# Eight-stream GNN stack on one core: masks of two score banks move from TensorE to VectorE, engine orders rewritten, loop unrolled

## What is computed

```python
h = jnp.maximum(_layernorm(x), 0.0); x = x + _L0_gnn_ref(h, ..., adj)   # masked attention, 8 heads of 32
h = jnp.maximum(_layernorm(x), 0.0); x = x + _L1_gnn_ref(h, adj, ...)   # (adj.T * q k^T) / row norm, times v
h = jnp.maximum(_layernorm(x), 0.0); x = x + _L2_gnn_ref(h, ..., adj)   # graph attention, softmax, elu
h = jnp.maximum(_layernorm(x), 0.0); x = x + _L3_gnn_ref(h, adj, ...)   # adj @ h @ w + bias
# inside L0:
attn = jnp.einsum('bhnd,bhmd->bhnm', q, k) * scale
attn = jnp.where(attn_mask[None, None] == 0, -jnp.inf, attn)
attn = jax.nn.softmax(attn, axis=-1)
o = o @ w_proj + b_proj; ...; return o + layernorm(o) * gamma + beta
```

## Time and profile before

| | us |
|---|---|
| median of 3 runs | 1529.49 |
| lowest and highest | 1529.12, 1531.04 |
| the profiled execution: its time | 1527.43 |
| the profiled execution: span, first to last instruction | 1525.4 |
| PE, DVE, ACT, POOL busy (share of the span) | 97%, 85%, 73%, 43% |

### The profile page before, as it was taken

How to read it: one execution, slowest core, us unless ns; L and a number is a source line. 1 busy time by engine, 2 the same in 40 slices (tenths; PEclk the granted TensorE clock), 3 DMA queues, 4 the chain that set the end, 5 groups by cost and what they waited for, 6 DMA issues and landing times.

```text
span 1525.4 us, 46270 instructions
## 1 busy us (share of the span) xinstructions
PE 1482.7 (97%) x16392; PEld 1375.0 (90%) x16392; DVE 1301.0 (85%) x3726; ACT 1120.1 (73%) x2884; POOL 661.3 (43%) x981
## 2 busy tenths in 40 slices
PE   6989999999999999999989999999999999999996
PEld 5879999999999999999989999999999999999985
DVE  3888888888888888888888898898898898898895
ACT  4667777777777777777767777777777777777763
POOL 2244444444444444444444444444444444444442
PEclk9999999999999999999999999999999999999999
DMA  3000010000000010000010010010000010000001
GB/s 107 15 16 15 23 30 22 23 29 22 23 30 22 23 29 22 23 29 23 23 31 18 28 29 18 27 30 18 28 30 19 26 30 20 25 29 22 17 16 35
DMA packets 38102, 39.84 MB, mean 26 GB/s; under 512 B 2416, under 2 KB 37488, under 8 KB 37872
## 3 DMA queue, kind: packets, MB, share of 16 engines
q1 hardware_dynamic: 37872, 36.84, 7.9%
HBM read 20.05 MB, written 16.78 MB: 24 GB/s over the span
## 4 chain that ended last, share of the span: by engine, by line
PE 94%; DVE 2%; issue 2%; ACT 1%; POOL 1%; DMA 0%; POOLq 0%; DVEq 0%; ACTq 0%
PE bank L325 41%; PE mid L360 7%; PE mid L325 6%; PE mid L372 5%; PE bank L384 4%; PE mid L388 4%; PE mid L365 4%; PE mid L446 4%; PE mid L534 4%; PE mid L423 4%; PE bank L341 3%; PE bank L474 3%; PE mid L341 2%; PE mid L452 1%; PE bank L458 1%
## 5 line engine op out<-in xcount | busy, mean ns | idle before, releaser
L557 ACT ACTIVATE probs<-mid,neg_max 128x128 f32<-128x128 f32 x1024 | 295.3, 423 | 49.9 <-DVE neg_max L797 49.9
L897 POOL TENSOR_TENSOR rstd<-var_eps,minus_half 128x2 f32<-128x2 f32 x320 | 244.0, 763 | 25.1
L927 POOL TENSOR_TENSOR xb<-x,b_proj_beta 128x512 f32<-128x512 f32 x64 | 82.7, 1293 | 283.1 <-DVE o_res L807 283.1
L895 POOL TENSOR_TENSOR var_eps<-mean_var,eps 128x2 f32<-128x2 f32 x320 | 104.2, 326 | 167.1 <-DVE mean_var L717 167.1
L912 POOL TENSOR_TENSOR inv_norm<-sum_sq,minus_half 128x2 f32<-128x2 f32 x64 | 44.1, 689 | 260.8 <-DVE sum_sq L772 260.8
L730 DVE SCALAR_TENSOR_TENSOR h_t_lo<-bank,h_t_hi 128x512 fp32r<-128x512 f32 x128 | 88.4, 691 | 79.1 <-ACT h_t_hi L650 55.4
L713 DVE BATCH_NORM_STATS2 stats<-x 128x6 f32<-128x256 f32 x384 | 143.3, 414 | 5.8 <-DMA x<-in_x 3.6
L360 PE MATMUL mid<-ident,probs 128*128 128x128 f32 x1024 | 144.0, 275 | 3.7 <-ACT probs L557 3.7
L724 DVE TENSOR_SCALAR z<-x,mean_var,rstd 128x256 f32<-128x256 f32 x384 | 141.2, 410 | 2.7 <-POOL rstd L897 2.7
L360 PEld LDWEIGHTS mid<-ident,probs 128*128 128x128 f32 x1024 | 117.7, 142 | 4.8 <-ACT probs L557 4.8
L384 PE MATMUL bank<-probs_t,v 128*32 128x128 f32 x2048 | 105.9, 278 | 6.6 <-issue 6.0
(11 more groups left out here) (149 smaller groups left out, 5649.5 us busy)
## 6 DMA issues: line engine op xcount, KB each, us to landing
x<-in_x SPq DMA_DIRECT2D x64, 256.0 KB, 2.7
out_x<-x SPq DMA_DIRECT2D x64, 256.0 KB, 2.2
w_qkv_sb<-in_w_qkv SPq DMA_DIRECT2D x1, 768.0 KB, 4.5
w_q_sb<-in_w_q SPq DMA_DIRECT2D x1, 256.0 KB, 4.4
w_k_sb<-in_w_k SPq DMA_DIRECT2D x1, 256.0 KB, 4.7
w_v_sb<-in_w_v_t SPq DMA_DIRECT2D x1, 256.0 KB, 5.6
w_proj_sb<-in_w_proj SPq DMA_DIRECT2D x1, 256.0 KB, 5.8
w_gat_x<-in_w_gat SPq DMA_DIRECT2D x1, 256.0 KB, 6.1
```

What stands on the lines that cost most here:

```text
L557: last = act.activation(probs[:, r, s], mid[:, r, s * N:(s + 1) * N], ACT.Exp, bias=neg_max[:, r, s:s + 1])
L895: pool.tensor_tensor(var_eps[:, k], mean_var[:, k, :, 1], eps[:], ALU.add).then_inc(ln_eps[k], 1)
L897: pool.tensor_tensor(rstd[:, k], var_eps[:, k], minus_half[:], ALU.pow).then_inc(ln_rstd[k], 1)
L927: pool.tensor_tensor(xb[:], x0[:, i1], both(b_proj_beta), ALU.add).then_inc(xb_ready, 1)
```

## The change

1. `scores`: the mask matmul is left for banks 0 and 1 only; for banks 2 and 3 the 16 score matmuls start their own accumulation. q is scaled by -SCALE, so all scores are negated; the mask is +1e30 and the maximum becomes a minimum; `exps` applies scale -1.
2. DVE: the `tensor_reduce` of banks 2 and 3 goes. In its place `least_masked(r)`, for r = 3 and r = 2: a one-column memset and four `tensor_tensor_reduce` of 128 columns, each adding the mask `mask` (float32, in SBUF) to a piece of the bank, writing the sum to SBUF (`masked`) and its minimum to `neg_max`. The other reduce (banks 0 and 1) stays. `exps(2)` and `exps(3)` read `masked`, not PSUM.
3. The loop is gone: all 71 steps are written out, semaphore values are constants; the number of waits per full step is that of the loop (`bank_free` keeps the first reader alone when all pairs exist).
4. `last_constants` on DVE and POOL, and `next_constants` on POOL, are made ahead of step 2; PE still waits for the last ones at step 5.
5. Orders. PE in a step, after: transposes of probs 0 and 2 (stream 2), u, sum of squares, hw, q, y_t, rel_v, s2, heads, v, z1, scores, y, z0, g, o, v1, z2, transposes 1 and 3 (stream 1), rel, att, k (stream 0). Before: u, heads, hw, k, y_t, sum of squares, s2, q, z1, rel_v, scores, o, g, v, y, v1, transposes 2 and 1, att, 3, z2, 0, rel, z0. DVE, ACT and POOL get new orders too. DVE after: o, relu_lo 0, moments of o, rel, o_gam, relu_lo 2, x1 and moments 1, x2_exp, sum_sq, x3_up, moments 0 and 3, x2, e_leaky, z1, y_lo, moments 2, e_neg_max, o_t, z0, relu_lo 1, least_masked(3), o_lo, the reduce of banks 0 and 1, z2, shift3, att_norm, x4, least_masked(2), o_res. Nearly every product gets another PSUM bank.
6. SP loads pair t in step t (before: pair t + 1), on the same two semaphores of pair t - 2. POOL's xb moves to stream 2 in its order.

```diff
@@ run
-            for t in range(FIRST):
+            for t in range(PAIRS + STREAMS - 1):
                 for made_by, make in set_up:
                     if made_by == t:
                         make()
-                step(t, t % 2, streams(t))
-            with eng.Fori(FIRST, PAIRS - STEPS + 1, STEPS) as t:
-                for i in range(STEPS):
-                    step(t + i if i else t, i % 2, [True] * STREAMS)
-            for t in range(PAIRS, PAIRS + STREAMS - 1):
                 step(t, t % 2, streams(t))
@@ scores
-                for r in range(RG):
+                for r in range(2):
                     pe.matmul(mid[:, r], ident_b[:], mask_b[:].unsqueeze(1).to_broadcast([128, BC, N]),
                               start=True, stop=False)
...
-                                             k_t[at, hc, b * N:(b + 1) * N], start=False, stop=s == BC - 1,
-                                             tile_position=(r * HD, 0))
+                                             k_t[at, hc, b * N:(b + 1) * N], start=r >= 2,
+                                             stop=r >= 2 or s == BC - 1, tile_position=(r * HD, 0))
@@ exps
-                    last = act.activation(probs[:, r, s], mid[:, r, s * N:(s + 1) * N], ACT.Exp,
+                    last = act.activation(probs[:, r, s], mid[:, r, s * N:(s + 1) * N] if r < 2 else masked[:, r - 2, s],
+                                          ACT.Exp, scale=-1.0,
                                           bias=neg_max[:, r, s:s + 1])
@@ VectorE
+            def least_masked(r):
+
+                dve.memset(mask_turn[:, r:r + 1], 0.0)
+                for s in range(BC):
+                    last = dve.tensor_tensor_reduce(out=masked[:, r - 2, s], in0=mid[:, r, s * N:(s + 1) * N], in1=mask[:],
+                                                    scale=1.0, scalar=LARGE, op0=ALU.add, op1=ALU.min,
+                                                    accum_out=neg_max[:, r, s:s + 1])
+                return last
...
-                    dve.tensor_reduce(neg_max[:, 2:4], mid[:, 2:4].rearrange("p r (s m) -> p r s m", m=N),
-                                      op=ALU.max, axis=AX.X, negate=True).then_inc(max_ready[1], 1)
...
+                    wait_before(dve, probs_ready[3], p1)
+                    least_masked(3).then_inc(max_ready[3], 1)
...
+                    wait_before(dve, probs_ready[2], p1)
+                    least_masked(2).then_inc(max_ready[2], 1)
...
-            run(dve, step, [(1, first_constants), (2, next_constants), (5, last_constants)])
+            run(dve, step, [(1, first_constants), (2, next_constants), (2, last_constants)])
...
-            run(pool, step, [(1, next_constants), (5, last_constants)])
+            run(pool, step, [(2, next_constants), (2, last_constants)])
```

More of the change, by code:

```diff
@@ L80, in gnn_stack @@
         mask_b = sb("mask_b", [128, N], bf16)
+        mask = sb("mask", [128, N])
         ones = sb("ones", [128, HD])
@@ L510, in step @@
+                    rows(halves(v1_bank), h_t[1], w_v_p, 0, D).then_inc(v1_psum, 1)
+                if on[4]:
+                    pe.wait_ge(z_ready[2], done(p4))
+                    bank_free(pe, (g_ready, p3, 1), (q_ready, p1, 1))
+                    transposes(z2_bank, z[2]).then_inc(h_t_psum[2], 1)
+                if on[1]:
                     pe.wait_ge(probs_ready[1], done(p1))
                     transpose_probs(1).then_inc(probs_t_psum[1], 1)
-                if on[5]:
-                    pe.wait_ge(att_norm_ready, done(p5, 2))
-                    bank_free(pe, (g_ready, p3, 1), (o_norm_ready, p2, 1))
-                    for b in range(2):
-                        last = pe.transpose(att_bank[:, b * N:(b + 1) * N], att_norm[:, b], ident[:])
-                    last.then_inc(att_t_psum, 1)
@@ L536, in step @@
                     last.then_inc(rel_psum, 1)
+                if on[5]:
+                    pe.wait_ge(att_norm_ready, done(p5, 2))
+                    bank_free(pe, (v1_ready, p3, 1), (h1_full_ready, p3, 1), (hw_ready, p5, 2))
+                    for b in range(2):
+                        last = pe.transpose(att_bank[:, b * N:(b + 1) * N], att_norm[:, b], ident[:])
+                    last.then_inc(att_t_psum, 1)
                 if on[0]:
-                    pe.wait_ge(z_ready[0], done(p0))
-                    bank_free(pe, (probs_t_ready[1], p1, 1))
-                    transposes(z0_bank, z[0]).then_inc(h_t_psum[0], 1)
-            run(pe, step, [(1, fold), (2, next_weights), (5, last_weights)])
+                    pe.wait_ge(h_lo_ready[0], done(p0))
+                    bank_free(pe, (o_ready, p2, 1), (max_ready[3], p1, 1), (x2_ready, p4, 2))
+                    columns(k_bank, w_qkv_p, D, h_t[0]).then_inc(k_psum, 1)
+            run(pe, step, [(0, fold), (2, next_weights), (5, last_weights)])
         @block.scalar
@@ L740, in step @@
                 i0, i1, i2, i3, i4, i5, i6, i7 = [(par + s) % 2 for s in range(STREAMS)]
+                if on[3]:
+                    dve.wait_ge(o_psum, done(p3))
+                    dve.tensor_tensor(o[:], pair_rows(o_bank), both(b_proj_bc), ALU.add).then_inc(o_ready, 1)
                 if on[1]:
                     relu_lo(0, p1, z0_bank)
+                if on[3]:
+                    dve.wait_ge(o_ready, done(p3))
+                    moments(LN_O, p3, o)
                 if on[4]:
@@ L749, in step @@
                        .then_inc(rel_ready, 1)
+                if on[3]:
+                    dve.wait_ge(ln_moments[LN_O], done(p3, 2))
+                    for b in range(2):
+                        last = dve.scalar_tensor_tensor(o_gam[:, b], o[:, b], mean_var[:, LN_O, b, 0:1], gamma_bc[:],
+                                                        ALU.subtract, ALU.mult)
+                    last.then_inc(o_gam_ready, 1)
+                if on[5]:
+                    relu_lo(2, p5, z2_bank)
+                if on[3]:
+                    dve.wait_ge(o_gam_ready, done(p3))
+                    dve.wait_ge(o_res_ready, done(p3))
+                    dve.wait_ge(ln_rstd[LN_O], done(p3))
+                    for b in range(2):
+                        dve.scalar_tensor_tensor(x1[:, i3, b], o_gam[:, b], rstd[:, LN_O, b:b + 1], o_res[:, b],
+                                                 ALU.mult, ALU.add).then_inc(x1_ready, 1)
+                    dve.wait_ge(x1_ready, done(p3, 2))
+                    moments(1, p3, x1[:, i3])
                 if on[6]:
```

490 lines of the change are left out of this document (233 added, 257 removed).

## The result

| | us |
|---|---|
| changed kernel, median of 4 runs | 1511.78 (1510.14 to 1512.36) |
| before, median of 4 runs beside them | 1529.3 (1527.46 to 1531.04) |
| ratio, 95% interval | 0.9886 (0.9872 to 0.9901) |
| profiled execution of after: span | 1508.4, before 1525.4 |

It is faster by 17.5 us. The forecast was 39.5 us (1490), its range 1474 to 1518: the direction came true, less than half of the size did.

A forecast was written before the change was run, and what follows sets the result against it. PE was taken to bound the kernel, before and after. Span 1525.4 - 28.2 - 4.5 - 6.0 = 1486.7, plus 4.1 to the median, = 1490.8; forecast 1490 us, range 1474 to 1518.

The forecast's parts named there:

- two masks fewer: PE's scores: two mask matmuls fewer save 0.44 us per pair, 28.2 us in all, for a step of 22.43 us.
- jump back: At the loop's only jump back a step took 4.54 us more; written out, this goes.
- late constants: Constants made ahead of step 2 remove PE's 6.01 us idle at step 5: -6 us, bounds -8 and 0.
- new neighbourhoods: Products standing beside other work in the full steps: 0, bounds 0.1 us per step either way, -6 to +6 us.
- ends: Filling and draining of the pipeline, as deep as before with 71 steps: 0, bounds -6 and +6 us.
- Loop: Written-out steps: -4.54 us once; a full step otherwise costs the same, 0 with bounds of 0.1 us per step.
- DVE's price: Fused instruction of 128 columns on DVE: 0.21 or 0.27 us, taken as 0.24; two memsets at 0.06 us each.
- The fit: DVE's work of 21.6 us fits in PE's step of 22.43, with 0.8 us of slack left (0.6 to 1.1).
- Rival 1: DVE's waits exceed its slack, so DVE and PE hold each other: 0.2 to 0.5 us per step, 1503 to 1522; chance 0.20.
- Rival 2: Fused instructions on DVE don't overlap, 0.5 us each; DVE sets a step of 23.7 us, 1572 us; chance of ending slower 0.09.
- Rival 3: A fixed wait in the new order takes back PE's saving, some 0.6 us per step: 1526 to 1532; chance 0.05.
- ACT: Eight exponentials on ACT read SBUF instead of PSUM, 394 ns against 423, so ACT gains time.

The follow-up runs named there:

- b_best: The kernel before with its order kept, loop written out, fused masks, late constants ahead of step 2, new tiles last in SBUF: 1488.77 us, ratio 0.9736.
- b_noloop: The kernel before with its loop alone written out; orders, masks and constants kept: 1523.06 us against 1528.43.
- a_place: The changed kernel with its three new SBUF tiles placed last, no instruction different: 1499.51 us in one run, 1497.95 us again in rounds, ratio 0.9798.
- b_pad32: The kernel before with one unused tile of 32 bytes at the place of mask_turn: 1543.44 us, one run.
- a_const5: The changed kernel with the late constants of DVE and POOL made at step 5 again: 1510.69 us, ratio 0.9877.
- m_dist: PE alone on zeros, eight groups of 12 product matmuls, activations' tile shifted by 0 to 512 bytes: k at shift 0 took 117.7 ns per matmul.
- m_entry: PE alone, groups k, q, v0, v1 at four shifts behind six pieces of work: 113.3 to 115.5 or 117.7 to 118.4 ns at shifts 0 and 128.

## Why the prediction was right or wrong

The sum, term by term, in us. The measured column is made from spans and mask distances, and ends at the span of 1508.4.

| term | forecast | measured | from |
|---|---|---|---|
| two masks fewer | -28.2 | -27.6 | 64 x (0.957 - 0.525) in PE's starts; b_best's step 22.43 |
| jump back | -4.5 | -4.5 | b_noloop |
| late constants | -6 (-8 to 0) | -8.1 | the step between the fourth and fifth masks: 27.79 before, 19.27 after, less 0.43 for the masks |
| new neighbourhoods: places in SBUF | 0 (with the next, -6 to +6) | +13.1 | 1508.4 - 1495.3, a_place_timed |
| new neighbourhoods: order of the groups | | +3.7 | 55 x (22.50 - 22.43) |
| ends | 0 (-6 to +6) | +6.3 | start +3.2, first eight steps +0.7, end +2.4, a_place_timed against b_best |

The forecast of the span was 1486.7. Against it the rows differ by 0.6 - 2.1 + 13.1 + 3.7 + 6.3 = 21.6, which gives 1508.3. The first three rows alone give 1525.4 - 27.6 - 4.5 - 8.1 = 1485.2; b_best, which has just these parts, has a span of 1485.3. The single rows are good to a microsecond or two: the two runs of a_place have spans of 1497.7 and 1495.3 at the same step of 22.50, and differ in the first steps and the last ones. For the places the full steps alone give 55 x 0.24 = 13.2 us.

- **The step that failed** is "Loop", where I took 0, with bounds of 0.1 us per step, for "the new neighbourhoods of products". I had thought of the order of the groups only. The three new tiles moved every operand behind them by 32 bytes more than a multiple of 256 against the weights, and from then on no group ran at 113 ns. It is 0.24 us a step, outside my bounds; b_pad32 brings it about without any other part of the change, a_place takes it away without undoing any other. The order, of which I had thought, adds 0.07 us a step.
- **Masks and jump back**: right in mechanism and size. With the addresses and the order of before, b_best's step is 22.43, the very number of the sum, and it took 1488.8 us where I forecast 1490.
- **Constants**: PE's idle time goes, the clock stays at 1.00 from 80 to 100 us, and the first three steps are no longer than before (49.6 us against 49.7). The size, 8.1, lay at the bound I had given. But most of the credit isn't the move's: with the new order and the constants at step 5 (a_const5) the step there is already 22.27, so the order brings 5.1 of the 8.1. The move brings 3.0 and costs 2.6 at step 2 (17.50 against 14.93), where I had put its cost at nothing. In the old order it is worth 8.4.
- **DVE's price**: 0.21 us per fused instruction, the lower of my two prices and not the 0.24 I took, and the memsets cost nothing. DVE's occupied time is 22.74 - 1.51 = 21.2 us instead of 21.6. The fit held with more room than forecast, and DVE's share is 89% instead of 91%. The Trainium skill's figure, from the page "VectorE: DVE Perf Modes", was an estimate of 0.26; the trace says 0.21.
- **Rival 1** (DVE and PE hold each other) gave a time, 1503 to 1522, that holds the result, but its mark is absent: PE shows no idle time behind a DVE release in any full step. A range can hold the time for a wrong reason. **Rival 2** needed 0.42 us per fused instruction; 0.21 were measured. **Rival 3** would have left 1526.
- **ACT**: I had read the earlier trace rows the wrong way round. They set exponentials of the softmax against others of another tile. With both sources in one line, those that read `masked` from SBUF take 438 ns and those from PSUM 398. These durations overlap and differ from kernel to kernel (423 from PSUM before, 388 and 372 in b_best); the distances of starts don't: 293 ns from SBUF and 249 from PSUM, in the changed kernel (44 ns more); b_best has 295 and 249. ACT had room, so it cost nothing. The Trainium skill, same page, section "The TRN2 errata", says that ScalarE instructions with an SBUF source run slower than specified, by a fixed cost each. The trace agrees that SBUF is the slower source; that the cost is a fixed one no run shows, since all have 128 columns.
- **The sentence that caught it** was the last of the prediction: the middle slower "for a reason that no DVE wait shows".
- **Ends**: with the new order (a_place_timed) the first masks start at 21.9 us, in b_best at 18.7. Two things stand between. The list of the change leaves out that PE's `fold`, a product of two weight matrices, moved from step 1 to step 0, ahead of the first transposes; the first product starts 15.15 - 13.37 = 1.8 us later. And 36 product matmuls, not 24, stand ahead of the first masks, since v comes before the scores: 6.7 us from first product to masks, 5.3 in b_best. That is the traces' account; no run has `fold` alone. Among all runs with the old order the first masks lie between 18.4 and 21.2, with the new one between 20.3 and 22.2, so a part of the 3.2 can be scatter. From the last masks to the end it is 77.9 to 80.9 us with the old order and 79.3 to 81.7 with the new one, so the 2.4 us there are within what runs of one order differ by.

PE's timeline of a_place_timed, then of b_best:

```profile
7.60 3.75 PE L387 MATMUL bank<-w_k_sb,w_q_sb 128*128 128x256 f32 x8 [7.60 <-DMA w_k_sb<-in_w_k]
...
15.15 0.58 PE L314 MATMUL mid<-h_t_hi,w_qkv_hi 128*128 128x256 f32 x1 [1.50 <-DVE h_t_lo L735]
```

```profile
7.82 2.99 PE L390 MATMUL bank<-w_k_sb,w_q_sb 128*128 128x256 f32 x8
...
13.37 0.55 PE L317 MATMUL bank<-h_t_hi,w_qkv_hi 128*128 128x256 f32 x1 [2.57 <-DVE h_t_lo L734]
```

## What to carry to other kernels

Where matmuls follow each other without a wait, their distance is a measure of its own: compare it per group, before and after, ahead of any story about waits. A new tile in the middle of the list moves all tiles behind it; put new tiles last, and when a change costs something that no wait shows, run the old kernel with unused tiles of the same sizes. Here the places alone were worth 13.8 us, nearly as much as the whole change brought; with the old order as well it is 1486 to 1489 us instead of 1512.

## What the runs showed of the hardware

- A product matmul of 256 columns follows the last one after 113.3 to 120.4 ns (means of groups), by the distance between the addresses of its weights and its moving operand, with a period of 256 bytes (m_dist), and by the work ahead of the group (m_entry). All means below 116 ns, in PE-only runs and whole kernels alike, stand at 64 or 192 bytes modulo 256. It is PE's alone: no other engine ran in m_dist and m_entry. Which part of PE it arises in stays open. The Trainium skill's page "SBUF — State Buffer", section "Who interferes with whom", gives PE two independent read ports, one for the moving operand and one for the weights, and says that "only the shared port pair causes contention", which is VectorE's and GpSimd's. The runs agree in that no other engine is needed for the cost, but differ where the two reads should be independent: in a kernel bound by PE, 32 bytes more between the two cost 14 us of 1529.
- Fused add-and-minimum instructions of 128 columns with a PSUM source start 0.21 us apart, at a duration of 0.29, with the reading of the accumulator between them.
- Exponentials of 128 columns on ACT start 249 ns apart from PSUM and 293 to 295 from SBUF (changed kernel and b_best).
- The busy share hides all of this: PE was at 660.00 of 660 us in before, after and b_best, with steps of 22.87, 22.74 and 22.43 us.
